# Inverse square roots in a layered attention and expert kernel: powers on GpSimd in place of Newton steps on VectorE

## The reference

```python
def _layernorm(x, axis=-1, eps=1e-05):
    m = jnp.mean(x, axis=axis, keepdims=True)
    v = jnp.var(x, axis=axis, keepdims=True)
    return (x - m) / jnp.sqrt(v + eps)
...
    def _features(x, omega, quad_nodes, quad_weights):
        xn = x / jnp.maximum(jnp.linalg.norm(x, axis=-1, keepdims=True), 1e-12)
        proj = jnp.einsum('bhtd,rhdm->rbhtm', xn, omega)
        arg = jnp.clip(proj * sqrt_2s - s, -20.0, 20.0)
        feat = jnp.exp(arg) / np.sqrt(M).astype(np.float32)
...
    x = _layernorm(x + _L0_attn_ref(...))
    x = _layernorm(x + _L0_ffn_ref(...))
    x = _layernorm(x + _L1_attn_ref(...))
    x = _layernorm(x + _L1_ffn_ref(...))
    return x
```

## Time and profile before

| | |
|---|---|
| median of 3 runs | 1610.31 us (1608.62 to 1610.74) |
| span of the profiled execution | 1609.7 us (no other time of this execution is shown) |
| TensorE busy | 1414.2 us (88%) |
| VectorE busy | 918.4 us (57%) |
| ScalarE busy | 683.3 us (42%) |
| GpSimd busy | 517.3 us (32%) |
| mean granted TensorE clock | 0.920 |
| attention, 331 to 872 us: PE, DVE, ACT, POOL busy | 466.02, 355.54, 209.88, 162.34 us of 541 |

### The profile page before, as it was taken

One profiled execution on the slowest core, in us unless ns is written; L12 is line 12 of the kernel. 1 busy time (PEld: TensorE's weight loads), 2 busy tenths in 40 slices (PEclk: granted clock), 3 DMA queues, 4 the chain that ended last, 5 costly groups with the idle time before them and its releaser, 6 DMA issues. The chain is left out here.

```text
span 1609.7 us, 34137 instructions
## 1 busy us (share of the span) xinstructions
PE 1414.2 (88%) x12248; PEld 1219.4 (76%) x12248; DVE 918.4 (57%) x1994; ACT 683.3 (42%) x1260; POOL 517.3 (32%) x395
## 2 busy tenths in 40 slices
PE   6799999759988989899893899899998999999990
PEld 5688888646766767666673788688888999999990
DVE  4766675747576765766664335334435555555544
ACT  2467566423443533435342323222223555555543
POOL 0245444322324334242300002343202444444440
PEclk7799999969999989999896899799998999999995
DMA  6233422120313223132103701224209888888865
GB/s 246 83 130 135 142 82 75 39 80 15 106 41 129 81 76 117 44 112 78 40 15 115 281 27 63 96 97 147 86 27 241 234 237 234 237 233 238 232 164 215
DMA packets 101207, 204.05 MB, mean 127 GB/s; under 512 B 18448, under 2 KB 72720, under 8 KB 94864
## 3 DMA queue, kind: packets, MB, share of 16 engines
q1 hardware_dynamic: 76032, 144.73, 27.5%
q0 software_dynamic: 23088, 54.31, 11.7%
q10 hardware_dynamic: 2016, 4.08, 0.7%
HBM read 144.53 MB, written 58.55 MB: 126 GB/s over the span
## 5 line engine op out<-in xcount | busy, mean ns | idle before, releaser
L2112 PE MATMUL e_ps<-e_xhl,e_whl 128*128 128x256 f32 x1872 | 248.9, 283 | 3.7 <-DMA e_whl<-wlo 3.7
L2112 PEld LDWEIGHTS e_ps<-e_xhl,e_whl 128*128 128x128 f32 x1872 | 233.7, 190 | 4.3 <-issue 4.3
L1703 PE MATMUL d_ps<-d_xhl,d_whl 128*128 128x512 f32 x768 | 195.3, 403 | 7.5 <-DVE d_whl L1773 5.3
L1703 PEld LDWEIGHTS d_ps<-d_xhl,d_whl 128*128 128x128 f32 x768 | 144.8, 194 | 38.5 <-issue 9.6
L2008 POOL DMA_INDIRECT xs<-e_y,e_slot_id x78 | 121.6, 1559 | 82.9 <-ACT e_y L2039 68.2
L1268 ACT ACTIVATE c_qf<-c_cf,fc 128x512 f32<-128x512 f32 x64 | 46.2, 721 | 221.3 <-DVE c_cf L1370 221.3
L382 POOL TENSOR_TENSOR b_hhl<-b_h,b_hhl 128x512 fp32r<-128x512 f32 x64 | 94.5, 1479 | 138.5 <-ACT b_hhl L609 112.2
L2092 PE MATMUL e_ps<-e_whl,e_ghl 128*128 128x256 f32 x936 | 137.7, 282 | 0.5 <-DVE e_ghl L2186 0.5
L2174 DVE TENSOR_TENSOR e_g<-e_ps,e_act_h 128x256 f32<-128x256 f32 x156 | 66.2, 425 | 115.4 <-ACT e_act_h L2053 96.1
L1878 DVE TENSOR_TENSOR d_g<-d_ps,d_act_h 128x512 f32<-128x512 f32 x64 | 44.2, 691 | 139.8 <-PE d_ps L1703 80.5
L2092 PEld LDWEIGHTS e_ps<-e_whl,e_ghl 128*128 128x128 f32 x936 | 120.5, 188 | 0.7 <-ACT e_ghl L2063 0.7
(11 more groups left out here) (304 smaller groups left out, 2647.7 us busy)
## 6 DMA issues: line engine op xcount, KB each, us to landing
e_whl<-wlo SPq DMA_DIRECT2D x39, 1024.0 KB, 5.0
e_whl<-wlo SPq DMA_DIRECT2D x39, 512.0 KB
c_eraw<-in_expert_w POOLq DMA_DIRECT2D x24, 512.0 KB, 4.7
wlo<-c_elo POOLq DMA_DIRECT2D x24, 512.0 KB, 3.0
wall<-in_expert_w SPq DMA_DIRECT2D x8, 1536.0 KB
xg<-b_zeros POOLq DMA_DIRECT2D x13, 780.0 KB, 3.9
e_xr<-xg SPq DMA_DIRECT2D x39, 260.0 KB
x<-rows_out SPq DMA_DIRECT2D x16, 512.0 KB, 3.1
```

Of the source, the lines that this page charges most:

```text
L1703: mm = pe.matmul(ps[:, H + 2 * (m % 2) + w, :], whl[:, wp, e, lo:lo + P], xhl[:, k, xp, kd, :], start=q == 0, stop=q == 3 * KD - 1)
L2112: mm = pe.matmul(ps[:, H + m, w * SLOT:(w + 1) * SLOT], whl[:, k, wp, lo:lo + P], xhl[:, k, xp, kd, :], start=q == 0, stop=q == 3 * KD - 1)
```

## The change

A constant tile `halves` (128x128, all -0.5) is set by GpSimd at the start of the attention. Both roots of the attention and the two of the last stage become a `tensor_tensor` on GpSimd with the operation `pow` and `halves` as exponent.

For the norms VectorE keeps the sums and the maximum with 1e-24 (`norms`, now in slot 5 with `norm_ready`); GpSimd takes the power and then multiplies. For the row scales VectorE ends with the variance (`var_ready`); GpSimd takes the power and the product with the mean (`row_roots`), with a wait for its own power between, at the end of its body. In the last stage GpSimd, which had no program there, does the same for each half. `phase_mixer` keeps its Newton rounds.

```diff
@@ phase_attention, gpsimd
+                    gp.wait_ge(s["norm_ready"], f + 1)
+                    gp.tensor_tensor(nrm[:, 1, :], nrm[:, 0, :], halves[:], ALU.pow).then_inc(s["rnorm_ready"], 1)
                     for c in range(KD):
                         gp.wait_ge(s["rnorm_ready"], f + 1)
...
+                if is_step(i - 1):
+                    row_roots(i)
+
+            def row_roots(i):
+                gp.wait_ge(s["var_ready"], i)
+                gp.tensor_tensor(small[:, 3, :], small[:, 2, :], halves[:, 0:BATCH], ALU.pow).then_inc(s["root_own"], 1)
+                gp.wait_ge(s["root_own"], i)
+                gp.tensor_tensor(small[:, 5, :], small[:, 0, :], small[:, 3, :], ALU.mult).then_inc(s["stats_ready"], 1)
+
+            gp.memset(halves[:], -0.5).then_inc(s["halves_set"], 1)
+            gp.wait_ge(s["halves_set"], 1)
@@ phase_attention, vector
-            def norm_guess(ch):
+            def norms(ch):
                 ch.wait()
-                ch.link(ve.tensor_scalar(nv, nv, 1e-24, None, ALU.max))
-                ch.link(ve.tensor_scalar(nrmi[:], nv.bitcast(I32), 1, None, ALU.logical_shift_right))
-                ch.link(ve.tensor_scalar(nr.bitcast(I32), nrmi[:], -1.0, float(0x5F3759DF), ALU.mult, ALU.add))
-
-            def norm_newton(ch, last):
-                ch.link(ve.scalar_tensor_tensor(nt, nr, -0.5, nr, ALU.mult, ALU.mult))
-                ch.link(ve.tensor_tensor(nt, nt, nv, ALU.mult))
-                ins = ve.scalar_tensor_tensor(nr, nt, 1.5, nr, ALU.add, ALU.mult)
...
+                ve.tensor_scalar(nv, nv, 1e-24, None, ALU.max).then_inc(s["norm_ready"], 1)
+                ch.end()
...
-                ch.link(ve.scalar_tensor_tensor(v, half_, 0.25, v, ALU.mult, ALU.add))
-
-            def row_scales(ch):
-                rsqrt(ch, v, r, t_, smalli[:])
-                ve.tensor_tensor(nb, mean, r, ALU.mult).then_inc(s["stats_ready"], 1)
+                ve.scalar_tensor_tensor(v, half_, 0.25, v, ALU.mult, ALU.add).then_inc(s["var_ready"], 1)
                 ch.end()
...
-                    if front and t == 6:
-                        norm_newton(norm, False)
...
-                    if front and t == 6:
-                        norm_newton(norm, True)
-                        norm.end()
...
                     if front and t == 5:
-                        norm_guess(norm)
-                        norm_newton(norm, False)
+                        norms(norm)
...
                     if back and t == 7:
                         row_moments(rows)
-                        row_scales(rows)
@@ phase_combine
+        @block.gpsimd
+        def _(gp):
+            for h in range(2):
+                tt = slice(h * HALF * BATCH, (h + 1) * HALF * BATCH)
+                gp.wait_ge(var_ready, h + 1)
+                gp.tensor_tensor(small[:, 3, tt], small[:, 2, tt], halves[:, 0:HALF * BATCH], ALU.pow).then_inc(root_own, 1)
+                gp.wait_ge(root_own, h + 1)
+                gp.tensor_tensor(small[:, 5, tt], small[:, 0, tt], small[:, 3, tt], ALU.mult).then_inc(scales_ready, 1)
...
-                ch.link(ve.scalar_tensor_tensor(v, half, 0.25, v, ALU.mult, ALU.add))
-                rsqrt(ch, v, r, t_, smalli[:, tt])
-                ve.tensor_tensor(nb, mean, r, ALU.mult).then_inc(scales_ready, 1)
+                ve.scalar_tensor_tensor(v, half, 0.25, v, ALU.mult, ALU.add).then_inc(var_ready, 1)
```

More of the change, by code:

```diff
@@ L901, in phase_mixer, with phase_attention @@
     nc.all_engine_barrier()
-def phase_attention(nc, x2, bqkv, bout, masks, x3, routed_w, wlo, ids, rows_out, x2_stored, x3_stored, early, x0, x0_in, fc):
+def phase_attention(nc, x2, bqkv, bout, masks, x3, routed_w, wlo, ids, rows_out, x2_stored, x3_stored, early, x0, x0_in, fc, halves):
     with ExitStack() as ctx:
@@ L922, in phase_attention @@
         va = sb("va", [P, BATCH, HEADS1, VP])
-        nrm = sb("nrm", [P, 3, BATCH * 2 * HEADS1])
-        nrmi = sb("nrmi", [P, BATCH * 2 * HEADS1], I32)
+        nrm = sb("nrm", [P, 2, BATCH * 2 * HEADS1])
         qkt = sb("qkt", [P, 2, 2 * KD, TOK], F32R)
@@ L951, in phase_attention @@
                  "score_done", "mask_done", "kt_done", "kr_ready", "pair_done", "state_new", "ot_ready", "xb_ready",
-                 "stats_ready", "out_ready", "stored", "norm_own", "ln_own", "bo_own", "pre_own")
+                 "stats_ready", "out_ready", "stored", "norm_own", "ln_own", "bo_own", "pre_own",
+                 "halves_set", "norm_ready", "var_ready", "root_own")
         s = {n: sem(n) for n in names if n != "stored"}
@@ L1381, in new_state @@
                 ve.tensor_tensor(held, ps[:, OB, SU:SU + BATCH * VP], held, ALU.add).then_inc(s["state_new"], 1)
-            nv, nr, nt = nrm[:, 0, :], nrm[:, 1, :], nrm[:, 2, :]
-            NORM_OWN = 3 + 2 + 3 * 3 - 1
+            nv = nrm[:, 0, :]
+            NORM_OWN = 2
             def squares(ch, f, half):
@@ L1390, in squares @@
                                          sq[:, 2 * half:2 * half + 2].rearrange("p b (n d) -> p (b n) d", d=HD), AX.X, ALU.add))
-            def norm_guess(ch):
+            def norms(ch):
                 ch.wait()
-                ch.link(ve.tensor_scalar(nv, nv, 1e-24, None, ALU.max))
-                ch.link(ve.tensor_scalar(nrmi[:], nv.bitcast(I32), 1, None, ALU.logical_shift_right))
-                ch.link(ve.tensor_scalar(nr.bitcast(I32), nrmi[:], -1.0, float(0x5F3759DF), ALU.mult, ALU.add))
-            def norm_newton(ch, last):
-                ch.link(ve.scalar_tensor_tensor(nt, nr, -0.5, nr, ALU.mult, ALU.mult))
-                ch.link(ve.tensor_tensor(nt, nt, nv, ALU.mult))
-                ins = ve.scalar_tensor_tensor(nr, nt, 1.5, nr, ALU.add, ALU.mult)
[L1402 to L1408, removed]
+                ve.tensor_scalar(nv, nv, 1e-24, None, ALU.max).then_inc(s["norm_ready"], 1)
+                ch.end()
+            mean, half_, v = (small[:, k, :] for k in range(3))
+            LN_OWN = 4 + 3 + 3
             def row_stats(ch, i):
@@ L2188, in _, with phase_combine @@
             in_turns(ve, GROUPS, body)
-def phase_combine(nc, xs, out):
+def phase_combine(nc, xs, out, halves):
     HALF = STEPS // 2
@@ L2204, in phase_combine @@
         small = sb("small", [P, 6, TILES])
-        smalli = sb("smalli", [P, TILES], I32)
         x_in = [sem(f"x_in{k}") for k in range(STEPS)]
-        own, scales_ready, by_act, by_dve, stored = (sem(n) for n in ("own", "scales_ready", "by_act", "by_dve", "stored"))
+        own, var_ready, root_own, scales_ready, by_act, by_dve, stored = (sem(n) for n in ("own", "var_ready", "root_own", "scales_ready", "by_act", "by_dve", "stored"))
         block = ctx.enter_context(nc.Block())
@@ L2254, in scales @@
                 tt = slice(h * HALF * BATCH, (h + 1) * HALF * BATCH)
-                mean, half, v, r, t_, nb = (small[:, k, tt] for k in range(6))
+                mean, half, v = (small[:, k, tt] for k in range(3))
                 ch.mark(ve.tensor_tensor(mean, stats[:, tt, 1], stats[:, tt, 4], ALU.add))
@@ L2303, in build_program @@
         rows_out = sb("rows_out", [P, BATCH, D])
+        halves = sb("halves", [P, BATCH * 2 * HEADS1])
         x2_stored, x3_stored, xs_stored, x0_in = (ctx.enter_context(nc.semaphore(n)) for n in ("x2_stored", "x3_stored", "xs_stored", "x0_in"))
```

6 lines of the change are left out of this document (2 added, 4 removed).

## The result

The change makes the kernel slower: 1741.87 us (1739.22 to 1742.59, 4 runs) against 1610.53 us (1608.62 to 1611.6, 4 runs) of the kernel before, a ratio of 1.0808, 95% interval 1.0794 to 1.0822. The forecast was 1586 us, the range 1573 to 1618. The span of the profiled execution is 1740.9 us, its mean granted clock 0.878 (0.920 before).

What follows compares the result with a forecast made beforehand. VectorE's root chains were taken to bind step ends, TensorE the middle. Six step ends of 3.0 us (18.0) plus 0.1, 2.0, 2.4 and 1.85 made 24.4 us off 1609.7: 1585.3, plus 0.6 gives 1586 us, range 1573 to 1618.

Steps and rivals of the forecast that it cites:

- X: Time of GpSimd's power of 128x128 for the norms, taken as 2.8 us: 11 passes at its multiply's rate plus 0.2 fixed.
- The upper bound: Highest time for GpSimd's 128x128 power: some 30 polynomial steps, each a whole pass, 7.3 us.
- the slow rival: GpSimd's norm power is slow and turns the sign: slower from 7.1 us, 1618 us at 8; chance 0.23.
- The replay: One attention step re-timed with the changed order: TensorE's norm transposes without a wait, 3.0 us gained at each of six step ends.
- The small powers: GpSimd's powers for row roots and last stage: 0.3 us for 4 elements, 0.5 us for 16.
- GpSimd's own wait: GpSimd's wait for its own previous instruction, between power and product, taken as 0.55 us.
- The row root's chain: From variance to ScalarE's normalising at a step's end: 1.25 us instead of 2.4.
- ScalarE's wait: ScalarE's wait before normalising at a step's end: some 2 us instead of 4.0.
- The last stage: VectorE's second statistics start 2.4 us earlier, ScalarE's next apply at 1599.5 instead of 1601.35: gain 1.85 us.
- Rival 1: In the attention TensorE waits for norms from GpSimd's slow power; 1618 us at 8 us, 1634 at 10; chance 0.23.
- turning point: Time of GpSimd's norm power at which the change goes from gain to loss: 7.1 us, 55 ns an element.
- Its line: Kernel time T = 1553.6 + 8X: each microsecond of power costs one at six step ends, step 0's end, before the first.

## Why the prediction was wrong

**The step that failed is the price of the power**, "I take X = 2.8 us: the root as VectorE does it is 11 passes" at GpSimd's rate for its multiply. It measured 20.8 us. The upper bound failed too: 30 passes at the multiply's rate gave 7.3 us "and no row excludes more", but the range ended at X = 8. The bound was made of two guesses, the number of passes and that a pass goes at the multiply's rate, and no row carried either. An unknown without a row should have given the slow rival more than 0.23, and a range open to that side. The price by column (16 partitions cost what 128 do) could not be read from any row of before.

The Trainium skill, GPSIMD Engine Reference, Performance pitfalls for Q7 kernels, was cited for 4 cycles an element and link of a dependent chain, from which an estimate of 25 links gave X = 10.7 and 1639 us. The runs show 20.8 us: the page pointed the right way, and its estimate was half the price. The same page's 6 us for the first call of a freshly loaded kernel (Instruction dispatch) did not show: the first power, at 342.06, takes 20.80 us like all others, and starts 0.08 us behind the end of the maximum.

**The replay held.** With X = 2.93 the ratio is 0.9843, which is the forecast's 1586 on its chip within 1 us; TensorE's transposes had no wait, and a step took 61.8 us in the mean ("62 to 63"). That it fits within 1 us is in part luck, since its parts were off in sizes that nearly cancel:
- The small powers: 1.01 us for 128x4 and 2.92 for 128x16, not 0.3 and 0.5.
- GpSimd's own wait: 0.08 us (601.49 to 601.57), not 0.55, which was the wait of a transfer that is issued behind a split. The row root's chain, from the variance's end to the normalising, is 600.40 to 601.88, 1.48 us and not 1.25; ScalarE's wait is 2.98 us ("some 2").
- The last stage: 0 and not 1.85 us, as its root and product take 3.28 us in place of 2.51. Run alone it is 1.0002.

**Rival 1 was what happened**, with its place (TensorE's wait for the multiplied norms) and its turning point (7.1 us, measured between 5.46 and 10.57). Its line is 22 us short at X = 20.8, for the most part since it let TensorE run at full clock behind the wait: the turns with a higher clock take back 2 us and more of the 3.2 us a step. The earlier trace rows already showed 0.57 to 0.66 behind waits of a few us; what comes behind a wait of 14 us (0.55 for 15 us) was left out of the line. Behind the attention the span grew by 3.2 us where the line had 1.9 us less, which no run assigns.

**What remains of the idea.** VectorE's chain of roots was on the path, as the profile of before said: taking the row roots off it gives 0.6%, and both roots, with ScalarE for the norms, 1.25%.

## What to carry to other kernels

Before an operation moves to another engine, its price there needs a row: if the trace has none of that kind, the bound from above is open, and a kernel of ten lines that times it at two sizes answers more than any count of passes. When a chain is to leave a crowded engine, cost the engine with a free slot and a fitting function (here ScalarE, 2.0 us) beside the one that merely has the most idle time. A wait put on TensorE costs more than its length where the clock is low behind it; here 2 to 3.5 us a time.

## What was not expected of the hardware

- A power on GpSimd costs 0.159 us a column and 0.43 us fixed, the same for 16 and 128 partitions and for exponents of -0.5 and 2.5; a product of 128x128 takes 0.454 us.
- Dependent instructions on GpSimd follow each other in 0.08 us: the product behind the power of 128x4, the multiplication behind the power of 128x128.
- Filler in TensorE's wait that left 4 to 7 us idle at its end did not bring the clock through: the four transposes behind took 1.11 us in most turns, 0.83 to 0.90 in three. With 0.8 us left they took 0.66 us; with 2.1 us left, in two turns, 0.82, and the contexts behind took 1.07 and not 0.66.
- With 72 or 112 instructions added to the loop's body, TensorE stood 2.5 to 4.2 us at the start of the next pass, in nine of ten turns, for nothing that the profile names; with 52 it did not.
- ScalarE loads a table each time it goes from logarithm to exponential and back, 1.28 us each; one of the two loads falls in idle time.
